# Perceiver block on Trainium2: cross-attentions with four-batch roots, summed head halves in the projection and joint key rotation

## The chip, the cores and the metric

The kernel runs on one NeuronCore of one Trainium2 chip. Its engines are TensorE (PE, with weight loads shown as PEld), VectorE (DVE), ScalarE (ACT), GpSimd (POOL) and SyncE (SP, which issues most DMAs). The metric is the device time of one execution in microseconds; lower is better.

## The reference

A block of six residual stages works on x of shape 32 x 32 x 256 (32 batches of 32 tokens). Two stages are cross-attentions to a context of 257 tokens for each batch, with 16 heads of 16 channels. These two are what the change touches.

```python
# stage 1: biases on q, k, v, o, and a mask
scores = q @ k^T / 4 + mask * -1e9          # per batch and head: 32 x 257
x = x + softmax(scores) @ v @ Wo + bo
# stage 4: no bias, no mask; q and k normed over 16 channels, then rotated
q = rope(q * rsqrt(mean(q*q) + eps) * wq);  k = rope(k * rsqrt(mean(k*k) + eps) * wk)
x = x + softmax(q @ k^T / 4) @ v @ Wo
```

Between and behind them stand a compressed self-attention with a Fourier transform, a plain self-attention and two layers of eight experts. All is float32.

## The kernel before, in words

Every engine has its own instruction stream, and the order in each is written by hand; semaphores join them. `cross(l)` is there for each engine, for the first (`l == 0`) and the second (`l == 1`) cross-attention. Its work goes in slots, one for each batch b = 4n + j (n = 0..7 groups of 128 tokens, j = 0..3). The two groups at each end are written out, and the ones between run in a hardware loop. In slot b the engines work on several batches at once, by the distances in `KEYS_AHEAD` and the constants beside it.

PE in slot b, in this order: turns probabilities of b, first half (`turns`, L685); scores of b+1 (`scores`, L671, which I use as the start of a slot); in slots with j = 1 the output projection of the four batches of group n-1 (`project`, L719); keys of a later batch, first half (`keys`, L617); `turns`, second half; `keys`, second half; for l = 1 the rotated keys of b+2 (`turn_keys`, L633, twice); values of b+1, first half (`values`, L649); weighted values of b (`weigh`, L702 and L706); `values`, second half. The two halves go through two PSUM banks, 6 and 7. Each matmul row of the trace holds two records for one matmul with 256 columns.

DVE in slot b: `merge` of b-1, which reads bank 5, where `weigh` left two head halves (L1560 multiplies by the share, L1563 adds the two halves, L1565 adds the value of the last, 257th context token); `shares` (L1539, L1542); for j = 1 `added` (L1572, the projection onto x, and L1578, statistics); `maxima` of b+1 (L1524 and L1528 for l = 0, L1530 for l = 1); then the copies of keys and probabilities out of PSUM (L1588, L1552, L1588). For l = 1 follow the sums of squares (L1601), every second slot the 12-step inverse root of two batches (L1630 to L1636), and the norm (L1619). A projection waits until `merge` of the batch with j = 0 of the next group has read bank 5, since it writes the same bank.

The context differs from its last token by `differ` (L2034, POOL), and POOL rotates keys for l = 1 (`rotate`, L1997 to L2001, four instructions for each half). ACT does exponentials (L1217) and the other copies. Before the slots of l = 0, DVE adds the output bias to x (L1656). The keys of the first batches of l = 1 are made early, while the results of the experts are gathered.

## Time and profile before

| | |
|---|---|
| median of three runs | 1277.69 us (1276.63 to 1279.93) |
| the profiled execution: its own time | 1276.58 us |
| its span in the profile | 1274.7 us |
| PE busy in the span | 996.5 us (78%) |
| DVE, ACT, POOL busy | 607.9, 494.9, 335.0 us |
| first cross-attention | from the start to about 251 us |
| second cross-attention | its early keys from 596 us, its slots from 675 to 951 us |

A busy share is a mean over stages with different limits. For a stage with slots, the length of one slot against the busy time of each engine in it says more: an engine that is busy for the whole slot sets its length, and where none is, the order of waits does.

### The profile page before, as it was taken

What the parts mean: (1) busy time and instruction counts of PE and PEld (TensorE: products, weight loads), DVE (VectorE), ACT (ScalarE), POOL (GpSimd) and SP (SyncE); (2) the same over time, 40 slices, a digit from 0 to 9 for tenths busy, and PEclk for the clock granted to TensorE, in tenths of its full rate; (3) what the DMA queues carried; (4) which work ended last, traced back from release to release, by engine and by line L of the source; (5) the groups of instructions that cost most, each with busy time, mean ns of one, the idle gap of its engine ahead of it and who ended that gap; (6) DMA issues with size and microseconds to landing.
All of it is one profiled execution on the core that took longest, in us unless ns stands there. A gap on an engine that the chain in (4) does not pass through costs nothing.

```text
span 1274.7 us, 24294 instructions
## 1 busy us (share of the span) xinstructions
PE 996.5 (78%) x8506; PEld 794.9 (62%) x8506; DVE 607.9 (48%) x1835; ACT 494.9 (39%) x1442; POOL 335.0 (26%) x494
## 2 busy tenths in 40 slices
PE   5999999888873899998147888888768875199990
PEld 3677667544652799997135656565548764199980
DVE  4555666513634011112775888888744554022222
ACT  3665666533330333322134555555545652011100
POOL 3111120002104000003527776777602100400004
PEclk9899999988985899999578999999986776599995
DMA  8111124000004788883100001100000000679953
GB/s 247 35 35 35 61 82 149 2 1 0 1 1 190 260 336 316 330 325 120 29 33 18 30 24 35 34 33 1 2 1 1 1 0 1 225 288 334 329 214 100
DMA packets 50562, 135.75 MB, mean 106 GB/s; under 512 B 16168, under 2 KB 37552, under 8 KB 44464
## 3 DMA queue, kind: packets, MB, share of 16 engines
q1 hardware_dynamic: 47408, 126.28, 27.8%
q0 software_dynamic: 3072, 8.39, 2.0%
q8 instruction: 49, 0.80, 0.2%
q14 instruction: 33, 0.27, 0.1%
HBM read 117.36 MB, written 17.30 MB: 106 GB/s over the span
## 4 chain that ended last, share of the span: by engine, by line
PE 60%; DVE 22%; issue 7%; ACT 3%; POOL 3%; SPq 2%; DMA 2%; DVEq 0%; another core or an unknown queue 0%; POOLq 0%; ACTq 0%
PE lower L1091 13%; PE upper L1100 9%; PE upper L649 6%; PE upper L617 5%; PE upper L850 3%; PE upper L685 3%; PE lower L671 2%; POOL xslot L2144 2%; PE upper L702 2%; PE lower L831 2%; PE upper L931 2%; DVE arena L1552 2%; PE upper L719 2%; DVE x L1960 1%; PE lower L566 1%
## 5 line engine op out<-in xcount | busy, mean ns | idle before, releaser
L1091 PEld LDWEIGHTS lower<-arena 128*128 128x128 f32 x1472 | 175.0, 195 | 6.1 <-DVE arena L1926 3.9
L1091 PE MATMUL lower<-arena 128*128 128x128 f32 x1472 | 176.0, 279 | 2.6 <-DVE arena L1926 2.6
L649 PE MATMUL upper<-wkv,arena 128*128 128x256 f32 x512 | 140.4, 398 | 12.0 <-ACT arena L1192 6.8
L1100 PE MATMUL upper<-arena 128*128 128x256 f32 x552 | 126.4, 379 | 0.0
L2150 POOL DMA_INDIRECT arena<-yslot,slot x32 | 30.7, 958 | 323.5 <-DMA yslot<-arena 314.3
L649 PEld LDWEIGHTS upper<-wkv,arena 128*128 128x128 f32 x512 | 90.5, 192 | 34.6 <-issue 12.3
L1100 PEld LDWEIGHTS upper<-arena 128*128 128x128 f32 x552 | 101.5, 190 | 12.0
L1450 ACT ACTIVATE arena<-lower,arena 128x128 f32<-128x128 f32 x184 | 52.5, 369 | 106.3 <-PE lower L1091 106.3
L1217 ACT ACTIVATE arena<-lower,arena 128x257 f32<-128x257 f32 x128 | 59.6, 474 | 60.2 <-DVE arena L1530 60.2
L2034 POOL TENSOR_TENSOR arena<-arena 128x512 f32<-128x512 f32 x64 | 70.6, 1114 | 36.4 <-ACT klast L1270 20.7
L685 PE MATMUL upper<-const,arena 128*128 128x128 f32 x512 | 77.8, 275 | 1.7 <-ACT arena L1227 1.4
L617 PE MATMUL upper<-wkv,arena 128*128 128x256 f32 x256 | 72.0, 412 | 6.3 <-DMA arena<-in_ctxT_dram 4.3
L1926 DVE COPY arena<-lower 128x256 f32<-128x256 f32 x46 | 19.3, 420 | 117.2 <-PE lower L1075 117.2
L685 PEld LDWEIGHTS upper<-const,arena 128*128 128x128 f32 x512 | 64.1, 142 | 17.1 <-ACT arena L1227 4.5
L617 PE MATMUL upper<-arena,wkv 128*128 128x257 f32 x256 | 68.6, 392 | 0.6 <-ACT vlast L1158 0.6
L1217 ACT ACTIVATE arena<-arena 128x257 f32<-128x257 f32 x128 | 63.7, 500 | 11.5 <-DVE arena L1528 10.9
L1203 ACT ACTIVATE arena<-upper 128x256 f32<-128x256 f32 x128 | 48.8, 381 | 48.5 <-PE upper L649 48.4
L2144 POOL DMA_INDIRECT xslot<-xn,slot x32 | 31.1, 973 | 133.1 <-DVE slot L1910 67.7
L1939 DVE COPY arena<-upper 128x256 f32<-128x256 f32 x46 | 19.5, 425 | 96.3 <-PE upper L1100 96.3
L617 PEld LDWEIGHTS upper<-wkv,arena 128*128 128x128 f32 x256 | 47.8, 203 | 21.0 <-issue 15.7
L566 PE MATMUL lower<-const,xn 128*128 128x128 f32 x96 | 20.4, 393 | 50.4 <-DVE xn L1499 50.4
L633 PE MATMUL upper<-const,arena 128*128 128x128 f32 x128 | 26.8, 299 | 38.1 <-DVE arena L1588 37.7
(236 smaller groups left out, 1885.1 us busy)
## 6 DMA issues: line engine op xcount, KB each, us to landing
arena<-in_ew_dram SPq DMA_DIRECT2D x23, 2048.0 KB, 7.2
arena<-in_ew_dram SPq DMA_DIRECT2D x23, 1536.0 KB, 6.1
arena<-in_ctxT_dram SPq DMA_DIRECT2D x16, 1028.0 KB, 5.1
xslot<-zero SPq DMA_DIRECT2D x2, 2944.0 KB, 15.4
arena<-xslot SPq DMA_DIRECT2D x46, 128.0 KB, 5.9
yslot<-arena SPq DMA_DIRECT2D x46, 128.0 KB, 6.2
const<-in_const_dram SPq DMA_DIRECT2D x1, 1154.0 KB, 7.6
x<-in_x_dram SPq DMA_DIRECT2D x1, 1024.0 KB, 5.7
```

Source lines behind the costliest of these rows:

```text
L566: ins = nc.tensor.transpose(bank[b][:, (2 * t + c) * P:(2 * t + c + 1) * P], xn[:, 2 * b + t, c * P:c * P + P], ident)
L617: ins = mm(o, a, v, start=(c == 0), stop=(c == KC - 1))
L649: ins = mm(bank[6 + w][:, 0:D], dctx[k2][:, c, j2, w * P:w * P + P], wkv[l][:, c, D:2 * D], start=(c == 0), stop=(c == KC - 1))
L685: ins = nc.tensor.transpose(bank[4][:, i * P:i * P + P], prob[j % 2][:, i, w * P:w * P + P], ident)
L850: ins = mm(bank[4 + j][:, c * 8 * T:(c + 1) * 8 * T], vq[k][:, j, c * P:c * P + P], spT[k][:, 2 * c:2 * c + 2, :], start=True, stop=True)
L1091: ins = mm(bank[1 + half][:, i * P:i * P + P], ew[k][:, at:at + P], exT[k % 2][:, c, :], start=(c == 0), stop=(c == KC - 1))
L1100: ins = mm(bank[4 + k % 2][:, 0:D], eh[k % 2][:, i, :], ew[k][:, at:at + D], start=(i == 0), stop=(i == nh - 1))
L1203: A(vb[j2 % 2][:, w, :], bank[6 + w][:, 0:D], copy).then_inc(q["vc"], 1)
L1217: A(prob[j2 % 2][:, i, :], src, ACT.Exp, bias=negmax[j2 % 2][:, i:i + 1], accum_out=rowsum[j2 % 2][:, i:i + 1]).then_inc(q["probs"], 1)
L1450: ins = A(eh[k % 2][:, c, :], bank[1 + half][:, i * P:i * P + P], ACT.Gelu_apprx_tanh, bias=eb1[k][:, c:c + 1])
L2034: G.tensor_tensor(dctx[k2][:, :, j2, :], of[:, :, 0:LASTKEY], of[:, :, LASTKEY:S].to_broadcast([P, KC, LASTKEY]), ALU.subtract).then_inc(q ...
L2144: G.indirect_dma_start(out=xslot[l], out_offset=at(i, t), in_=xn[:, t, :], in_offset=None)\
```

## The change

It makes seven edits. (1) `merge` is one multiplication: the two head halves are no longer added, but both are multiplied by the output weights and summed in PSUM, so a projection has four matmuls in place of two. (2) The last token's value is no longer added in `merge`: before the slots, 16 matmuls (`last_outputs`) multiply all last values by the output weights, the result with the bias goes to the new tile `vwo`, and a fifth matmul with four contraction rows adds it in each projection. The bias is no longer added to x. (3) The root of the key norms is made once for four batches, keys are made eight slots ahead in place of six (`DIFF_AHEAD` and `SUMS_AHEAD` go to seven), and `kraw` is doubled. (4) POOL rotates both key halves with four instructions in place of eight. (5) PE makes the second half of the values ahead of `weigh`. (6) DVE does `shares` and `maxima` ahead of `merge`, and `added` after the copy of the turned probabilities; PE does the first half of the keys ahead of the projection. (7) One semaphore covers the last keys' load and the mask and bias loads.

```diff
-        KEYS_AHEAD = (2, 6)
-        DIFF_AHEAD = (2, 5)
-        SUMS_AHEAD, NORM_AHEAD, ROPE_AHEAD, TURN_AHEAD = 5, 4, 3, 2
+        KEYS_AHEAD = (2, 8)
+        DIFF_AHEAD = (2, 7)
+        SUMS_AHEAD, NORM_AHEAD, ROPE_AHEAD, TURN_AHEAD = 7, 4, 3, 2
...
+                def last_outputs():
+                    for b in range(4):
+                        for t in range(2):
+                            n = 2 * b + t
+                            for c in range(KC):
+                                ins = mm(bank[b][0:QB, t * D:t * D + D], vlast[l][:, c, QB * n:QB * n + QB], wo[l][:, c, :],
+                                         start=(c == 0), stop=(c == KC - 1))
+                        ins.then_inc(q["lastvals"], 1)
...
                     for c in range(KC):
-                        ins = mm(bank[5][:, 0:D], attended[k][:, c, :], wo[l][:, c, :], start=(c == 0), stop=(c == KC - 1))
-                    ins.then_inc(q["ow"], 1)
+                        for e in range(2):
+                            mm(bank[5][:, 0:D], attended[k][:, c, e, :], wo[l][:, c, :], start=(c == 0 and e == 0), stop=False)
+                    mm(bank[5][:, 0:D], const[0:QB, C_TOKB:C_TOKB + P], vwo.rearrange("j n d -> j (n d)")[:, bass.ds(n * D, D)],
+                       start=False, stop=True).then_inc(q["ow"], 1)
...
 # PE, slot
                     scores(n, k, j, it)
+                    keys(n, k, j, it, 0)
                     if there(n):
                         project(n, k, j)
-                    keys(n, k, j, it, 0)
...
                     values(n, k, j, it, 0)
+                    values(n, k, j, it, 1)
                     weigh(n, k, j, it)
-                    values(n, k, j, it, 1)
...
 # DVE, merge
-                    V.tensor_tensor(pairs.rearrange("p c e q -> p (c e q)"), bank[5][:, 0:P], parts_of, ALU.mult)\
-                     .then_inc(q["merge"], 1)
-                    dve.wait_ge(q["merge"], 2 * b + 1)
-                    V.tensor_tensor(merged, pairs[:, :, 0, :], pairs[:, :, 1, :], ALU.add).then_inc(q["merge"], 1)
-                    dve.wait_ge(q["merge"], 2 * b + 2)
-                    V.tensor_tensor(attended[k][:, :, T * j:T * j + T], merged,
-                                    vlast[l][:, :, bass.ds(b, 1)].to_broadcast([P, KC, T]), ALU.add).then_inc(q["outc"], 1)
+                    V.tensor_tensor(attended[k][:, :, :, T * j:T * j + T],
+                                    bank[5][:, 0:P].rearrange("p (c e q) -> p c e q", c=KC, e=2),
+                                    parts_of.rearrange("p (c e q) -> p c e q", c=KC, e=2), ALU.mult).then_inc(q["outc"], 1)
...
 # DVE, slot
+                    shares(n, k, j, it)
+                    maxima(n, k, j, it)
                     if there(n0):
                         merge(n0, k0, j0)
-                    shares(n, k, j, it)
+                    keys(n, k, j, it, 0)
+                    turned(n, k, j, it)
                     if j == 1 and there(n) and not (isinstance(n, int) and n == 0):
                         added(n - 1)
-                    maxima(n, k, j, it)
-                    keys(n, k, j, it, 0)
-                    turned(n, k, j, it)
                     keys(n, k, j, it, 1)
...
 # before the slots of l = 0, DVE
-                    dve.wait_ge(mask_loaded, 16 * (QB + 1))
+                    dve.wait_ge(mask_loaded, 16 * (QB + 1 + KC))
                     mine(V.tensor_scalar(negmask[:, :], negmask[:, :], -1e9, None, ALU.mult))
-                    for t in range(NT):
-                        ins = V.tensor_tensor(x[:, t, :], x[:, t, :], bo_bc[:, :], ALU.add)
-                    mine(ins)
+                    for b in range(4):
+                        dve.wait_ge(q["lastvals"], b + 3)
+                        V.tensor_tensor(vwo[:, 2 * b:2 * b + 2, :], bank[b][0:QB, :].rearrange("j (n d) -> j n d", d=D),
+                                        bo_bc[0:QB, :].unsqueeze(1).to_broadcast([QB, 2, D]), ALU.add).then_inc(q["vwc"], 1)
```

How instructions stand on PE before, in the slot of batch 5 (j = 1) of the first cross-attention, from its scores on; arena holds the working tiles, upper and lower are the PSUM banks 4 to 7 and 0 to 3:

```order
L671 MATMUL lower<-arena 64x257 x8
L719 MATMUL upper<-wo,arena 128x256 x2
L617 MATMUL upper<-arena,wkv 128x257 x2
L685 MATMUL upper<-const,arena 128x128 x4
L617 MATMUL upper<-arena,wkv 128x257 x2
L649 MATMUL upper<-wkv,arena 128x256 x2
L702 MATMUL upper<-arena 32x64 x16
L706 MATMUL upper<-const,arena 32x128 x4
L649 MATMUL upper<-wkv,arena 128x256 x2
```

And the same slot in the changed kernel, with its own line numbers:

```order
L680 MATMUL lower<-arena 64x257 x8
L624 MATMUL upper<-arena,wkv 128x257 x2
L729 MATMUL upper<-wo,arena 128x256 x4
L730 MATMUL upper<-vwo,const 128x256
L694 MATMUL upper<-const,arena 128x128 x4
L624 MATMUL upper<-arena,wkv 128x257 x2
L656 MATMUL upper<-wkv,arena 128x256 x4
L711 MATMUL upper<-arena 32x64 x16
L715 MATMUL upper<-const,arena 32x128 x4
```

The projection (L719, now L729 and L730) has five matmuls in place of two and stands behind the first keys; all values stand ahead of the weighing.

On DVE before, around the merge that this projection waits for (L1560 to L1565), up to the first of the maxima of the same slot (L1522, L1524):

```order
L1552 COPY arena<-upper 128x512
L1560 TENSOR_TENSOR arena<-upper,arena 128x128
L1563 TENSOR_TENSOR arena<-arena 128x64
L1565 TENSOR_TENSOR arena<-arena,vlast 128x2x32
L1539 RECIPROCAL arena<-arena 128x4
L1542 TENSOR_TENSOR arena<-const,arena 128x128
L1572 TENSOR_TENSOR x<-x,upper 128x256
L1578 BN_STATS ln_stats<-x 128x6
L1522 MEMSET spare 1x1
L1524 ISA arena<-lower,negmask 128x257
```

And in the changed kernel, from the second half of that slot's maxima on:

```order
L1540 MEMSET spare 1x1
L1542 ISA arena<-lower,negmask 128x257
L1542 ISA arena 128x1
L1542 ISA arena<-lower,negmask 128x257
L1542 ISA arena 128x1
L1546 TENSOR_SCALAR arena<-arena 128x2
L1578 TENSOR_TENSOR arena<-upper,arena 128x4x32
L1570 COPY arena<-upper 128x512
L1586 TENSOR_TENSOR x<-x,upper 128x256
L1592 BN_STATS ln_stats<-x 128x6
```

The merge, now one instruction (L1578), stands behind all maxima of the slot, and the addition to x behind the copy of the turned probabilities.

## Rows read from the trace of the kernel before

**Rows 1.** Stretches, first cross-attention: length; busy PE, PEld, DVE, ACT, POOL; clock; DMA.

```profile
124.20:132.02 7.82, 7.08 (x85) 5.38 (x84) 4.38 (x21) 4.35 (x15) 0.00 (x0) 1.00 0.33 107
132.02:139.24 7.22, 6.23 (x82) 4.63 (x81) 4.92 (x19) 4.56 (x15) 5.19 (x6) 1.00 0.09 33
139.24:145.39 6.15, 6.15 (x82) 4.60 (x81) 3.63 (x18) 4.27 (x15) 0.00 (x0) 1.00 0.01 4
69.53:239.62 170.09, 160.80 (x2029) 120.77 (x2028) 102.63 (x465) 108.73 (x351) 26.98 (x31) 1.00 0.20 68
```

**Rows 2.** The same view, second cross-attention.

```profile
825.73:837.09 11.36, 7.96 (x90) 5.66 (x89) 8.22 (x23) 4.77 (x16) 8.04 (x14) 1.00 0.15 45
844.27:852.94 8.67, 7.02 (x86) 4.90 (x85) 6.90 (x17) 4.76 (x16) 7.59 (x14) 1.00 0.00 0
852.94:860.04 7.10, 6.80 (x85) 4.97 (x84) 6.72 (x17) 4.75 (x16) 5.35 (x9) 1.00 0.00 0
683.36:894.15 210.79, 178.97 (x2121) 128.54 (x2120) 176.63 (x457) 118.97 (x376) 152.07 (x260) 0.99 0.08 26
894.15:946.83 52.68, 39.12 (x517) 26.88 (x516) 32.83 (x86) 27.48 (x88) 20.27 (x37) 0.94 0.01 2
```

**Rows 3.** Timeline of PE, first cross-attention: start, length, work, idle before.

```profile
124.81 1.13 PE L719 MATMUL upper<-wo,arena 128*128 128x256 f32 x4
...
140.83 0.60 PE L685 MATMUL upper<-const,arena 128*128 128x128 f32 x4
141.26 1.03 PE L617 MATMUL upper<-arena,wkv 128*128 128x257 f32 x4
142.13 1.03 PE L649 MATMUL upper<-wkv,arena 128*128 128x256 f32 x4
```

**Rows 4.** Timeline of DVE, the same slot as the last three rows.

```profile
142.17 0.69 DVE L1552 COPY arena<-upper 128x512 f32<-128x512 f32 x1
144.35 0.29 DVE L1560 TENSOR_TENSOR arena<-upper,arena 128x128 f32<-128x128 f32 x1 [1.49 <-ACT arena L1235]
```

**Rows 5.** Timeline of PE and DVE, second cross-attention.

```profile
806.35 0.44 PE L633 MATMUL upper<-const,arena 128*128 128x128 f32 x2 [0.30 <-DVE arena L1588]
...
806.92 0.20 DVE L1630 TENSOR_SCALAR root_v<-arena 128x64 f32<-128x64 f32 x1
...
809.94 0.69 DVE L1619 TENSOR_TENSOR arena<-arena 128x512 f32<-128x512 f32 x1
...
822.70 0.89 DVE L1630 TENSOR_SCALAR root_v<-arena 128x64 f32<-128x64 f32 x1
...
828.69 1.13 PE L719 MATMUL upper<-wo,arena 128*128 128x256 f32 x4 [2.27 <-DVE arena L1565]
...
829.98 0.42 DVE L1572 TENSOR_TENSOR x<-x,upper 128x256 f32 x1 [0.86 <-PE upper L719]
```

**Rows 6.** Timeline of the program's start, and of the last keys' matmuls.

```profile
22.10 0.99 PE L578 MATMUL upper<-ctxl,wkv 128*128 128x32 f32 x8
...
24.31 1.09 DVE L1654 TENSOR_SCALAR negmask<-negmask 128x257 f32<-128x257 f32 x1 [11.10 <-DMA bo_bc<-in_bo_dram]
...
25.43 6.86 DVE L1656 TENSOR_TENSOR x<-x,bo_bc 128x256 f32<-128x256 f32 x8
...
28.50 1.28 ACT L1217 ACT_TABLE_LOAD   x1
...
34.85 2.07 PE L649 MATMUL upper<-wkv,arena 128*128 128x256 f32 x4 [5.15 <-ACT arena L1171]
...
590.97 1.05 PE L585 MATMUL upper<-wkv,ctxl 128*32 128x256 f32 x4
```

**Rows 7.** Timelines around the second cross-attention: POOL and PE.

```profile
669.01 0.46 POOL L1997 TENSOR_TENSOR arena<-arena,ropew 128x128 f32<-128x128 f32 x1 [15.59 <-DVE arena L1619]
...
673.75 1.19 POOL L2040 TENSOR_TENSOR arena<-qT,const 128x256 f32<-128x256 f32 x2
...
916.06 1.48 PE L649 MATMUL upper<-wkv,arena 128*128 128x256 f32 x4 [2.73 <-ACT arena L1192]
```

More of the change, by code:

```diff
@@ L245, in perceiver_block @@
         vb = [ar.take(KW2, D) for _ in range(2)]
-        kraw = [ar.take(KW2, D) for _ in range(QB)]
+        kraw = [[ar.take(KW2, D) for _ in range(QB)] for _ in range(2)]
         ksq = [ar.take(KW2, D) for _ in range(2)]
@@ L249, in perceiver_block @@
         krope = [ar.take(KW2, D) for _ in range(2)]
-        ka = ar.take(D)
-        kb = ar.take(D)
+        ka = ar.take(KW2, D)
+        kb = ar.take(KW2, D)
         lraw, lsq = ar.take(D), ar.take(D)
-        kss = ar.take(2 * KW2, NH)
-        kr = ar.take(2 * KW2, NH)
+        kss = ar.take(QB * KW2, NH)
+        kr = ar.take(QB * KW2, NH)
         lss, lr = ar.take(NH), ar.take(NH)
         assert ar.at < 21024
+        probT = [ar.take(KW2, 4, P) for _ in range(2)]
+        parts_of = ar.take(P)
+        assert ar.at < 21536
         ar.at = 21536
         xq = [ar.take(KC, QB, 2, T) for _ in range(2)]
-        attended = [ar.take(KC, P) for _ in range(2)]
+        attended = [ar.take(KC, 2, P) for _ in range(2)]
         prob = [ar.take(4, S) for _ in range(2)]
@@ L262, in perceiver_block @@
         xsmall = ar.take(64)
-        ar.at = 18000
-        probT = [ar.take(KW2, 4, P) for _ in range(2)]
-        pairs = ar.take(KC, 2, T)
-        merged = ar.take(KC, T)
-        parts_of = ar.take(P)
-        assert ar.at < 21024
         negmax = [xsmall[:, 4 * i:4 * i + 4] for i in range(2)]
@@ L665, in scores @@
                         after(pe, q["probs"], 4 * b2)
+                    if isinstance(b2, int) and b2 == 0:
+                        pe.wait_ge(q["vwc"], 4)
                     if j2 == 0:
@@ L747, in cross @@
                     last_values()
[L748 removed]
+                    pe.wait_ge(q["lastvals"], 2)
                     pe.wait_ge(q["qc"], 4)
+                    last_outputs()
                     slots(pe, slot, -KEYS_AHEAD[l])
@@ L768, in cross @@
                     turn_last_keys()
+                    last_outputs()
                     slots(pe, slot, 1 - EARLY, -1)
                     pe.wait_ge(q["qrope"], 1)
+                    pe.wait_ge(q["vwc"], 4)
                     for b in range(4):
@@ L1246, in slot @@
                     values(n, k, j, it, 0)
+                    values(n, k, j, it, 1)
                     shared(n, k, j, it)
-                    values(n, k, j, it, 1)
                 if l == 0:
@@ L2010, in rotate @@
                     after(pool, q["tw"], KW2 * (b2 - 1))
-                    for w in range(KW2):
-                        after(pool, q["krope"], KW2 * b2 + w)
-                        rope(krope[j2 % 2][:, w, :], kn[j2 % 2][:, w, :], P, rope_k(w), "krope", KW2 * b2 + w + 1)
+                    after(pool, q["krope"], b2)
+                    rope(krope[j2 % 2], kn[j2 % 2], P, 0, KW2, "krope", b2 + 1)
                 def last_column(n, k, j, it):
```

68 lines of the change are left out of this document (35 added, 33 removed).

## The prediction, made before the changed kernel ran

> **What bounds the kernel now.** I read the view of busy time by stretch first, with stretches cut from one batch's scores to the next. In the first cross-attention a plain slot takes 6.15 us and PE is busy for 6.15 of them: PE alone sets it. The slot with j = 1 takes 7.82, and j = 2, where POOL works 5.19 us beside it, 7.22; PE has gaps there [rows 1]. So a group of four takes 27.3 us, of which PE's stream is 4 x 6.15 + 0.97 for the projection. In the second cross-attention a group takes 34.2 us (11.36, twice some 7.1, and 8.67) and PE is busy for only about 28 [rows 2]. There the timeline shows PE waiting for DVE: 2.27 us ahead of the projection, 0.30 ahead of the turned keys, and more in slots that follow a root [rows 5]. DVE's long pieces there are the roots, 3.02 us from the first step to the norm where nothing disturbs them [rows 5]. So an edit that shortens DVE pays in the second cross-attention, and one that lengthens PE, or puts something ahead of what PE waits for, costs in the first.
>
> **First cross-attention, slots.** Times are from the start of a slot's scores.
>
> The projection: two matmuls with 256 columns stand 0.87 apart from the next two (141.26 to 142.13), so one is 0.435, and 0.10 is added where short matmuls follow [rows 3]. Five are 2.27, where two are 0.97: +1.30. The fifth has only four contraction rows. Its price is not in the trace; I bound it between nothing and 0.435 and take 0.435, since its columns are those of the others. The Trainium skill, "TensorE: Matmul & The Clock Gate" (Why this matters for your kernels), says that a single matmul with 32 contraction rows takes the time of one with 128; by it the sum stays as it is, and no row here shows it for four rows. If it were free, 14 projections would return 6 us.
>
> Its wait: before, `merge` is long done, and the projection starts 0.61 after the scores (124.81) [rows 1, 3]. Now the merge follows the maxima. These end 2.93 into the slot (142.17 less 139.24), the multiplication is 0.32 with its gap (0.29 busy), and DVE to PE takes about 0.14: the projection starts at 3.4 [rows 1, 4]. The first keys, moved ahead of it, cover PE only until 1.59 (140.83) [rows 3]. So PE idles 1.8. The values are now four long matmuls in a row, which saves one change of 0.10. The slot is 6.15 - 0.10 + 2.27 + 1.8 = 10.1, in place of 7.7 in the mean (170.09 less five of 7.22 and 13 of 6.15, over seven). Nothing hides this: turns, keys, values and weighing all stand behind the projection on PE.
>
> The j = 2 slot: before, weighing waited for DVE's copy of the turned probabilities, which now comes 0.32 later (merge in between), but no second half of the values follows the weighing: 7.22 + 0.32 - 0.97 = 6.6. The other slots: 6.05. There the copy ends at about 3.9 and PE reaches the weighing at 4.7, so moving the merge costs nothing; without that cover it would cost 0.3 a slot.
>
> From slot 5 to slot 30 (170.09 us, 25 slots) there are seven projections, five j = 2 slots with POOL's burst and 13 others: 7 x 10.1 + 5 x 6.6 + 13 x 6.05 = 182.4: **+12.3** [rows 1]. The last projection's five matmuls (+1.3) are met by two DVE instructions fewer (-0.6) and two slots without values behind the weighing (-0.7): 0.
>
> **First cross-attention, start.** Now DVE's additions to x (6.86 us until 32.3) hold the first maxima, and the first exponential starts 1.0 later, at 33.3 [rows 6]. They go. But PE's last values move from 22.10 behind the bias load (24.3), and 16 matmuls of 0.435 follow (7.0; the two of the last keys, with 32 columns of weights, took 1.05). ACT's table load came 6.4 after the last values' start (28.50); now it comes at 24.3 + 7.0 + 6.4 = 37.7 and ends 1.28 later, so the first exponential is at 39.0: +5.7 [rows 6]. Against it: PE idled 5.15 us before 34.85, and its next matmuls ran at half pace (2.07 where 1.03 is usual) with the turns and scores behind them I put the loss at 2.2 [rows 3, 6]. The 16 matmuls fill that gap. Net **+3.5** (bounds +1.6, if the table is loaded before the keys' copy, and +5.7).
>
> **Second cross-attention.** Early keys: two batches more. PE's four groups at 0.87 are 3.5, and the root, now over 128 elements, costs 0.8 more (a step on 64 elements is 3.02 / 12 = 0.25 with its gap, one on 128 is 0.32, as the multiplication of the merge) [rows 3 to 5]. DVE goes on to the experts' sum only after this work: **+4.3** (0 if the gathers were the later, 9 if the stalls between the early copies grow with them).
>
> Handover: POOL waited 15.59 us and began a rotation at 669.01, behind the root that DVE made after the queries; its eight instructions took until 673.75, and only then were the queries spread that the first scores need [rows 7]. That root (3.0) is now made early, and the joint rotation takes some 4.0 in place of 4.74: **-3.8** (0 to -4.3). POOL's start after the last keys' copy moves by 7 us of `last_outputs` and of four copies, under DVE's work on the queries.
>
> Slots: no root in j = 2 any more, so j = 3 falls from 8.67 to the others' length. A plain slot: DVE's merge is 0.32 later than the maxima, but its copies had waited for PE, so PE's second turned keys move only by 0.16; behind them 0.10 is saved: 7.15, as now (7.10) [rows 2, 5]. j = 1: the root starts at 4.3 of the j = 0 slot and takes 3.8, the norm 0.6: until 1.55 of the next slot. Shares 0.7, maxima 1.2, merge 0.3: the projection starts at 3.85 (2.96 now, 828.69) and takes 2.27. Then a turn 0.44, its copy on DVE 0.7, the addition with statistics 0.95 (two instructions on 256 elements; the first is 0.42), the key copy 0.5, and 3.44 of PE behind it (a plain slot, 7.15, less the 3.7 at which its second turned keys start): 12.1, against 11.36 [rows 2, 5]. The 25 slots of 210.79 us become 5 x 12.1, one of 8.5 (root, no projection), 18 x 7.15 and one of 6.2 (keys are done sooner): 203.9: **-6.9** [rows 2]. Of the last stretch (52.68) the stall of 2.73 before 916.06, which the last root caused, goes with its cold clock (-3.3), two projections grow (+1.2 and +2 at the lower clock), and ends shrink by 1.0: **-1.1** [rows 2, 7].
>
> **Sum.** 12.3 + 3.5 + 0 + 4.3 - 3.8 - 6.9 - 1.1 = +8.3, against the profiled execution's own 1276.58: 1284.9. That execution lies 1.1 under the median, so 1286.
>
> **Rivals.**
> 1. The second cross-attention becomes bound by PE (faster). DVE's work in a group falls from 28.4 busy by about 5; if its copies then always came ahead of PE, a slot is PE's own 6.7 (7.10 less the wait of 0.30 and the 0.10 saved) and all 25 take 25 x 6.7 + 5 x 2.27 = 179 in place of 204: 1261 [rows 2, 5]. For it: roots are what delays the j = 3 slot. Against: PE's second turned keys still stand behind scores, maxima, merge and two copies of their own slot. It decides where 12 of those 25 us come, with a plain slot at 6.9 or less and no wait ahead of the projections. That half gives 1274.
> 2. The preludes cost nothing (no change). If the last outputs and the early keys lie in gaps that exist anyway (5.15 us of PE idle at the start, the gathers of the experts' results), 7.8 goes: 1278.
> 3. Longer POOL instructions hold DVE up (slower yet). One root step took 0.89 beside a POOL instruction where it takes 0.20 [rows 5]. I expect POOL to be through before the root starts; if not, about 1.2 for each of six roots: 1293. The Trainium skill, "SBUF — State Buffer" (SBUF: two separate sides), says that DVE and GpSimd take a shared port pair for a whole instruction, and the other waits; the 0.89 agrees, and by it joint rotations of over 1 us make each collision longer.
>
> **Numbers.** Forecast 0.50; rival 1 0.18; rival 2 0.17; rival 3 0.15. Predicted time 1286. The range of 1273 to 1295 takes in rival 2, rival 3 and the bounds of the preludes, and leaves most of rival 1 out. What a measurement tells from no change here is 0.3%, 3.8 us. Slower 0.65 (forecast and rival 3), same 0.17, faster 0.18.
>
> **What would show it.** In the changed profile: first cross-attention j = 1 slots of 10 us with PE idle some 1.8 ahead of L729, released by DVE's L1578; its other slots at 6.05; the first exponential near 39 us; in the second, j = 1 near 12.1, j = 3 near 7.15, and the projection 3.9 after the scores. The forecast is wrong if the projections of the first cross-attention start within 2 us of their scores, if the five matmuls take well under 2.2 us, or if plain slots of the second fall below 6.9.

## The result and the profile after

The changed kernel takes 1294.43 us in the median of 4 runs (1290.01 to 1295.11), the kernel before 1277.16 (4 runs, 1273.87 to 1279.93): a ratio of 1.0129, 95% interval 1.0095 to 1.0162. The change makes the kernel 17 us slower. The forecast was slower by 8 (1286, range 1273 to 1295).

The view of busy time by stretch, the changed kernel, cut from scores to scores as before; first the slot of batch 13 (j = 1), the j = 2 slot behind it, a plain one, and the 25 slots from the sixth on, all of the first cross-attention:

```profile
core 0: us, PE busy (x) PEld busy (x) DVE busy (x) ACT busy (x) POOL busy (x), PEclk, DMA share, GB/s
133.19:143.39 10.20, 8.87 (x91) 6.20 (x90) 3.97 (x18) 4.44 (x14) 0.00 (x0) 1.00 0.17 53
143.39:149.99 6.60, 6.38 (x82) 4.53 (x81) 4.91 (x16) 4.43 (x14) 5.18 (x6) 1.00 0.21 83
156.34:162.52 6.18, 6.18 (x81) 4.52 (x80) 3.18 (x16) 4.29 (x14) 0.00 (x0) 1.00 0.00 0
75.07:259.01 183.94, 173.97 (x2072) 124.83 (x2071) 92.51 (x414) 109.41 (x350) 26.96 (x31) 1.00 0.18 63
```

Against [rows 1] the j = 1 slot is 10.20 in place of 7.82, the j = 2 slot 6.60 in place of 7.22, and the 25 slots 183.94 in place of 170.09. The timeline of the j = 1 slot (start, duration, engine, line; in brackets the idle time before it and its releaser) shows why:

```profile
135.93 0.29 DVE L1578 TENSOR_TENSOR arena<-upper,arena 128x128 f32<-128x128 f32 x1
...
136.27 2.00 PE L729 MATMUL upper<-wo,arena 128*128 128x256 f32 x8 [1.33 <-DVE arena L1578]
...
138.20 0.69 PE L730 MATMUL upper<-vwo,const 4*128 x2
...
138.82 0.66 PE L694 MATMUL upper<-const,arena 128*128 128x128 f32 x4
```

The projection starts 3.08 after its scores, released by the merge (L1578), which now stands behind the maxima; its five matmuls hold PE until the next turn at 138.82, 2.55 us. The second cross-attention, the same view: the slot of batch 1, a j = 1 slot, a plain one, the slot of batch 25, and the 25 slots from the first on:

```profile
713.38:723.74 10.36, 8.57 (x85) 5.80 (x84) 8.05 (x16) 4.75 (x15) 8.48 (x10) 0.84 0.01 2
778.76:791.07 12.31, 9.53 (x96) 6.63 (x95) 6.98 (x18) 4.75 (x15) 7.21 (x9) 1.00 0.01 1
798.20:805.38 7.18, 6.76 (x85) 4.90 (x84) 4.41 (x10) 4.75 (x15) 5.69 (x8) 1.00 0.40 133
914.24:929.87 15.63, 12.13 (x88) 8.19 (x87) 6.77 (x16) 4.34 (x14) 7.31 (x9) 0.67 0.00 0
706.32:914.24 207.92, 184.79 (x2143) 132.93 (x2142) 140.56 (x336) 118.72 (x376) 133.46 (x161) 0.98 0.07 24
```

The 25 slots are 2.9 shorter than in [rows 2] (210.79): the j = 3 slots are 7.1 in place of 8.67, the j = 1 slots 12.3 in place of 11.36, and the last stretch is longer (below).

Where the 17.3 us between the two profiled spans (1274.7 and 1292.0) lie, cut at PE's landmarks in both timelines (scores, and the transposes behind each layernorm):

| Stretch | before | after | difference | forecast |
|---|---|---|---|---|
| start, to the sixth slot's scores | 69.53 | 75.07 | +5.5 | +3.5 |
| first cross-attention, 25 slots | 170.09 | 183.94 | +13.9 | +12.3 |
| its end, to the transposes | 20.08 | 20.33 | +0.2 | 0 |
| first self-attention | 113.28 | 111.43 | -1.9 | 0 |
| experts, to the last values | 217.09 | 217.10 | 0 | 0 |
| last values and early keys, to the transposes | 43.75 | 51.96 | +8.2 | +4.3 |
| queries, to the first slot's scores | 49.54 | 46.49 | -3.1 | -3.8 |
| second cross-attention, 25 slots | 210.79 | 207.92 | -2.9 | -6.9 |
| its last slots, to the transposes | 56.38 | 58.39 | +2.0 | -1.1 |
| second self-attention | 116.86 | 112.05 | -4.8 | 0 |
| the rest | 207.31 | 207.32 | 0 | 0 |

The two self-attention stages are the same code in all kernels here. Over the 14 profiles of this study the first takes 111.4 to 116.1 and the second 111.1 to 116.9, without any tie to the edits: I take -1.9 and -4.8 for that spread and not for a gain of the change. With one profile of each kernel this is not settled.

### The profile page after: what moved, and what is told of

It reads as the page before. It is cut to its first block, busy times and chain, and to the rows that moved or that the text cites. A ratio compares the mean times of both kernels' runs of the same rounds, so it can differ in the third digit from the quotient of the medians.

```text
span 1292.0 us, 24163 instructions
## 1 busy us (share of the span) xinstructions
PE 1040.5 (81%) x8666; PEld 814.5 (63%) x8666; DVE 542.8 (42%) x1607; ACT 497.8 (39%) x1446; POOL 316.9 (25%) x366
## 4 chain that ended last, share of the span: by engine, by line
PE 63%; DVE 15%; issue 10%; POOL 4%; ACT 4%; SPq 2%; DMA 1%; another core or an unknown queue 1%; DVEq 0%; POOLq 0%; ACTq 0%
PE lower L1105 13%; PE upper L1114 9%; PE upper L656 7%; PE upper L694 4%; PE upper L624 4%; PE upper L729 3%; PE lower L680 3%; PE upper L711 3%; PE upper L864 2%; DVE arena L1548 2%; PE upper L945 2%; PE lower L845 1%; DVE arena L1602 1%; DVE arena L1736 1%; ACT arena L1351 1%
## 5 line engine op out<-in xcount | busy, mean ns | idle before, releaser
L656 PE MATMUL upper<-wkv,arena 128*128 128x256 f32 x512 | 126.5, 388 | 7.1 <-ACT arena L1206 4.4
L656 PEld LDWEIGHTS upper<-wkv,arena 128*128 128x128 f32 x512 | 93.7, 192 | 25.7 <-ACT arena L1185 6.8
L694 PE MATMUL upper<-const,arena 128*128 128x128 f32 x512 | 82.0, 283 | 2.0 <-ACT arena L1241 1.4
L624 PE MATMUL upper<-wkv,arena 128*128 128x256 f32 x256 | 74.0, 422 | 11.9 <-issue 5.3
L2049 POOL TENSOR_TENSOR arena<-arena 128x512 f32<-128x512 f32 x64 | 66.0, 1043 | 48.9 <-ACT klast L1288 33.4
L694 PEld LDWEIGHTS upper<-const,arena 128*128 128x128 f32 x512 | 57.5, 142 | 27.4 <-issue 17.8
L624 PEld LDWEIGHTS upper<-wkv,arena 128*128 128x128 f32 x256 | 48.6, 208 | 30.2 <-issue 21.9
L1570 DVE COPY arena<-upper 128x512 f32<-128x512 f32 x64 | 43.6, 682 | 51.6 <-PE upper L694 51.6
L1548 DVE TENSOR_REDUCE arena<-lower 128x2 f32<-128x514 f32 x64 | 41.3, 686 | 55.3 <-PE lower L680 55.3
L1542 DVE CUSTOM_DVE_ANT_0 arena<-lower,negmask 128x257 f32<-128x257 f32 x128 | 49.0, 420 | 27.5 <-PE upper L694 24.0
```

Source lines behind the costliest of these rows:

```text
L624: ins = mm(o, a, v, start=(c == 0), stop=(c == KC - 1))
L656: ins = mm(bank[6 + w][:, 0:D], dctx[k2][:, c, j2, w * P:w * P + P], wkv[l][:, c, D:2 * D], start=(c == 0), stop=(c == KC - 1))
L694: ins = nc.tensor.transpose(bank[4][:, i * P:i * P + P], prob[j % 2][:, i, w * P:w * P + P], ident)
L1542: V.tensor_tensor_reduce(prob[p][:, i, :], bank[i][:, 0:S], negmask[:, :], 1.0, float(np.finfo(np.float32).min), ALU.add, ALU.max, rowmax[ ...
L1548: V.tensor_reduce(negmax[p][:, two], lower[:, two, 0:S], AX_X, ALU.max, negate=True)\
L1570: V.tensor_copy(probT[j % 2][:, 1, :, :].rearrange("p i q -> p (i q)"), bank[4][:, :]).then_inc(q["turnc"], 1)
```

## The experiments

All were timed in turns with the kernel before on the same chip; a ratio below 1 is faster than before. The kernel before took 1274.38 in the turns of the first four kernels of the table and 1276.8 to 1277.0 in the others, so kernels of different turns are best compared by their ratios. "Slots" is the time from the first slot's scores to those of the 26th in the second cross-attention (before 210.79, after 207.92).

| Kernel | median us | ratio, 95% interval | slots |
|---|---|---|---|
| the change, merge first | 1264.33 | 0.9926 (0.9901 to 0.9950) | 195.46 |
| the change, two matmuls | 1267.89 | 0.9953 (0.9934 to 0.9972) | 200.26 |
| before, keys' part | 1306.98 | 1.0256 (1.0233 to 1.0279) | 237.90 |
| before, values' order | 1278.43 | 1.0032 (1.0013 to 1.0052) | 215.09 |
| before, joint rotation | 1308.40 | 1.0239 (1.0213 to 1.0266) | 240.93 |
| before, root per four | 1266.06 | 0.9926 (0.9899 to 0.9953) | 202.57 |
| hybrid | 1249.32 | 0.9784 (0.9766 to 0.9802) | 195.45 |
| merge first, four early | 1268.11 | 0.9928 (0.9907 to 0.9949) | 195.36 |
| hybrid, separate rotation | 1254.19 | 0.9817 (0.9785 to 0.9850) | 197.22 |
| joint rotation, merge in PSUM | 1263.04 | 0.9898 (0.9869 to 0.9928) | 203.49 |
| hybrid, late gathers | 1253.27 | 0.9814 (0.9786 to 0.9841) | 195.59 |
| before, root per four and order | 1259.82 | 0.9878 (0.9845 to 0.9912) | 206.19 |

### 1. Is it the merge's place? (the change, merge first)

```
 # DVE, slot
+                    if there(n0):
+                        merge(n0, k0, j0)
                     shares(n, k, j, it)
                     maxima(n, k, j, it)
-                    if there(n0):
-                        merge(n0, k0, j0)
                     keys(n, k, j, it, 0)
```

> The changed kernel with one edit: DVE does the merge's one multiplication first in a slot, ahead of the shares and the maxima, as the kernel before did; the five-matmul projection, its place behind the first keys and all else stay. Theory (the projections wait for the late merge): the first cross-attention's slots with a projection fall from 10.2 to 8.8 us (the projection starts 1.65 after its scores, when the first keys are through, in place of 3.08), 7 of them: -10; the second's fall from 12.3 to 10.9 where the root does not hold DVE longer, 6 of them: -8. Together 1276, within 3. Rival (the merge's place costs nothing in sum): the maxima of every slot come 0.3 later, exponentials and weighing with them, 60 slots of which half pay, and the result stays within 0.3% of the changed kernel's 1294.

Measured 1264.33: 30 us less than the changed kernel (27 when each is set against the kernel before of its own turns), and faster than before. Busy time by stretch (the slot of batch 13, a j = 1 slot and batch 25's of the second cross-attention, its 25 slots), and PE's projection in the timeline of batch 25:

```profile
131.83:140.44 8.61, 8.61 (x92) 6.29 (x91) 3.98 (x19) 4.44 (x14) 0.00 (x0) 1.00 0.20 60
770.19:780.88 10.69, 9.53 (x96) 6.63 (x95) 7.14 (x17) 4.75 (x15) 7.21 (x9) 1.00 0.01 2
896.89:905.90 9.01, 7.65 (x87) 5.28 (x86) 5.74 (x14) 4.23 (x14) 5.90 (x8) 1.00 0.00 0
701.43:896.89 195.46, 181.82 (x2143) 131.18 (x2142) 140.84 (x337) 118.74 (x376) 131.89 (x161) 1.00 0.08 26
```

```profile
898.69 1.99 PE L729 MATMUL upper<-wo,arena 128*128 128x256 f32 x8 [1.11 <-DVE arena L1578]
```

In the first cross-attention the j = 1 slot falls by 1.6 and PE is busy for all of it. In the second it falls by 1.6 too. The plain slots are 7.06 for the most part (7.09 before this edit). The rival's price isn't paid there: the merge starts 0.14 before the slot's scores, in time in which DVE stood anyway, and the maxima start as long after the scores as before the edit (the last of them after 1.41 in plain slots of the second cross-attention). Only in its j = 1 slots, where the root holds DVE until then, do most of them come 0.7 later. The gain is 12 us beyond the expectation: the slots of batch 1 and 21 fall by 1.8 and 3.3 (their clock is no longer under 0.9), and above all the slot of batch 25 takes 9.01, not 15.63. In the changed kernel its projection looks like this:

```profile
916.10 0.83 DVE L1560 TENSOR_TENSOR arena<-const,arena 128x128 f32<-128x128 f32 x1
916.86 1.28 DVE L1548 TENSOR_REDUCE arena<-lower 128x2 f32<-128x514 f32 x2
918.06 0.27 DVE L1578 TENSOR_TENSOR arena<-upper,arena 128x128 f32<-128x128 f32 x1
...
918.39 3.78 PE L729 MATMUL upper<-wo,arena 128*128 128x256 f32 x8 [3.45 <-DVE arena L1578]
...
922.10 1.22 PE L730 MATMUL upper<-vwo,const 4*128 4x256 f32 x2
```

PE idles 3.45 us, and its next matmuls go at half pace: 3.78 where 2.00 is usual (granted clock 0.67 over the slot, so most of it at 1.2 GHz, the lower of the two levels). With the merge first PE idles 1.11 there, and the clock stays at 1.00. So here the wait is paid twice, once as idle time (2.3 of the 6.6 us) and again in the matmuls behind it: from batch 25's scores to the transposes behind the layernorm the changed kernel takes 58.39 and this one 51.01. The second price is not fixed by the length of the wait, as the next kernel shows.

### 2. What do three matmuls cost? (the change, two matmuls)

```
-                        for e in range(2):
-                            mm(bank[5][:, 0:D], attended[k][:, c, e, :], wo[l][:, c, :], start=(c == 0 and e == 0), stop=False)
-                    mm(bank[5][:, 0:D], const[0:QB, C_TOKB:C_TOKB + P], vwo.rearrange("j n d -> j (n d)")[:, bass.ds(n * D, D)],
-                       start=False, stop=True).then_inc(q["ow"], 1)
+                        ins = mm(bank[5][:, 0:D], attended[k][:, c, 0, :], wo[l][:, c, :], start=(c == 0), stop=(c == KC - 1))
+                    ins.then_inc(q["ow"], 1)
```

> The changed kernel with a projection of two matmuls: it leaves out the second halves of the heads and the last values with the output bias (the merge's product for both halves, the last outputs and all waits stay). It measures what three more matmuls cost. Theory (PE has nothing beside them, everything in the slot stands behind): 2.55 falls to 0.97, so -1.58 for each of 16 projections: -25, to 1269. Rival (in the second cross-attention DVE sets the slot, so the matmuls are hidden there): only the first's 8 projections pay, -12.6, to 1282.

Measured 1267.89. The first cross-attention's j = 1 slots fall from 10.20 to 8.58, the full 1.6. In the second they are 10.86, 11.73, 10.58 and 11.79 in place of 12.49, 12.31, 12.22 and 12.25: two of four fall by the full 1.6, two by a third of it. The stretches of batch 9, 13 and 25 tell why:

```profile
767.15:778.88 11.73, 9.57 (x90) 6.85 (x89) 7.09 (x18) 4.76 (x15) 7.21 (x9) 0.85 0.00 0
800.28:810.86 10.58, 7.89 (x90) 5.66 (x89) 6.94 (x18) 4.76 (x15) 7.21 (x9) 1.00 0.01 4
896.62:907.70 11.08, 7.58 (x81) 5.42 (x80) 6.77 (x16) 4.24 (x14) 6.11 (x8) 0.85 0.01 1
```

```profile
900.76 1.86 PE L728 MATMUL upper<-wo,arena 128*128 128x256 f32 x4 [3.45 <-DVE arena L1576]
```

The two longer slots have a granted clock of 0.85 and 0.86, where the changed kernel had 1.00: they save the three matmuls too, and lose 1.1 of it to the clock. So the matmuls are not hidden in the second cross-attention. Batch 25's slot is 11.08 in place of 15.63, of which the three matmuls are only a part. PE waits 3.45 for the merge as in the changed kernel, and the clock falls behind it here too (1.86 for two matmuls that take 1.13 elsewhere), but for less long: 0.85 over the slot, not 0.67. That brings the last stretch from 58.39 to 51.67, and the total near the expected 1269 is in part this luck. The same wait was thus followed by a short and by a long time at the lower clock, and a wait of 1.86 ahead of batch 9's projection by none in the changed kernel and by some here. What decides it, the runs don't show.

### 3. What is the keys' part worth? (before, keys' part; joint rotation; root per four)

The first of the three puts both edits into the kernel before, the other two one each: `KEYS_AHEAD` 8 with `DIFF_AHEAD` and `SUMS_AHEAD` 7 and `kss`, `kr` and the root over `QB * KW2`, or the rotation

```
-                    for w in range(KW2):
...
-                        rope(krope[j2 % 2][:, w, :], kn[j2 % 2][:, w, :], P, rope_k(w), "krope", KW2 * b2 + w + 1)
...
+                    rope(krope[j2 % 2], kn[j2 % 2], P, 0, KW2, "krope", b2 + 1)
```

> The kernel before with the keys' part of the change alone: keys eight batches ahead, one root per four batches, both halves of a batch's keys rotated together. Theory: the early keys cost 8 to 9 more (two more batches in straight-line code beside the gathers), the handover to the queries gives 2 to 4 back, and in the second cross-attention the j = 3 slots lose 1.5 each (six of them: -9) while the root ahead of j = 1 grows by 0.8 (+5) and the tail gives 3: in sum 1275 to 1280, no difference that can be told. Rival A (POOL's longer instructions hold DVE's roots up): 1285 or more. Rival B (the keys' part is the good part, and the early keys' cost is met elsewhere): 1270 or less.

> The kernel before with one part of the change: both halves of a batch's keys are rotated together on POOL (four instructions of up to 1.27 us in place of eight shorter ones); keys stay six ahead, a root per two batches. Theory (a POOL instruction holds up DVE's instructions that have both operands and the result in SBUF, for as long as it runs; the joint ones are longer and fall on DVE's merge and shares): the second cross-attention's slots grow, though by less than in the kernel with eight keys ahead, 0.5 to 1 in each of 25: 1285 to 1300. Rival (the joint rotation is shorter in sum and harmless, the loss of the kernel with all of the keys' part came from the root over four batches or from keys eight ahead): 1272 to 1277.

> The kernel before with the other part: keys eight batches ahead and one root per four batches; the halves of the keys are still rotated one after the other. Theory (the joint rotation is what made the keys' part 32 us slower): early keys +9, fewer roots -9, root ahead of j = 1 +5, handover -2: 1278 to 1284. Rival (the root over four batches, or where it falls against POOL's work, is the cause): 1295 or more.

Measured 1306.98, 1308.40 and 1266.06. The two halves of the same part have opposite signs: the joint rotation alone costs 31 us, the root per four batches alone gives 11. With both, the kernel is as slow as with the first, so that beside roots per four batches the joint rotation costs over 40. None of the three theories was met in size: "no difference" for the sum was wrong by 30 us, the joint rotation cost more than its 0.5 to 1 a slot (1.2), and the roots per four gave 11 where a small loss was expected. The time of the first is that of its rival A, but not for rival A's reason: in its slots no root step takes over 0.3. The groups of instructions of DVE in the slots show what happens (mean ns behind the comma): first the kernel before, then the joint rotation.

```profile
L1542 DVE TENSOR_TENSOR arena<-const,arena 128x128 f32<-128x128 f32 x25 | 13.9, 556 | 1.0
L1565 DVE TENSOR_TENSOR arena<-arena,vlast 128x64 f32<-128x64 f32 x24 | 9.3, 387 | 2.3
L1563 DVE TENSOR_TENSOR arena<-arena 128x64 f32<-128x64 f32 x24 | 8.0, 332 | 0.8
```

```profile
L1542 DVE TENSOR_TENSOR arena<-const,arena 128x128 f32<-128x128 f32 x25 | 25.6, 1026 | 1.0
L1565 DVE TENSOR_TENSOR arena<-arena,vlast 128x64 f32<-128x64 f32 x24 | 21.4, 892 | 2.3
L1563 DVE TENSOR_TENSOR arena<-arena 128x64 f32<-128x64 f32 x24 | 21.0, 874 | 0.8
```

The shares (L1542) and the merge's two additions (L1563, L1565) are the same instructions on the same tiles, and take 1.8 to 2.6 times as long. DVE's busy time in the 25 slots rises from 176.63 to 206.13, by 29.5; the slots grow by 30.1. The timeline of one slot of the kernel with joint rotations sets the two engines side by side:

```profile
833.23 0.73 POOL L1999 TENSOR_TENSOR arena<-arena,ropew 128x256 f32<-128x256 f32 x1 [6.99 <-DVE arena L1619]
833.24 0.80 DVE L1563 TENSOR_TENSOR arena<-arena 128x64 f32<-128x64 f32 x1
...
833.91 0.73 POOL L2000 TENSOR_TENSOR arena<-arena,ropew 128x256 f32<-128x256 f32 x1
...
834.16 0.56 DVE L1565 TENSOR_TENSOR arena<-arena,vlast 128x64 f32<-128x64 f32 x1
...
834.60 1.27 POOL L2001 TENSOR_TENSOR arena<-arena,ropew 128x512 f32<-128x512 f32 x1
834.64 0.17 DVE L1539 RECIPROCAL arena<-arena 128x4 f32<-128x4 f32 x1
834.84 1.17 DVE L1542 TENSOR_TENSOR arena<-const,arena 128x128 f32<-128x128 f32 x1
...
835.94 1.28 DVE L1530 TENSOR_REDUCE arena<-lower 128x2 f32<-128x514 f32 x2
835.95 1.26 POOL L2003 TENSOR_TENSOR arena<-arena 128x512 f32<-128x512 f32 x1
```

Each of the three DVE instructions ends with the POOL instruction beside it (834.04 and 833.96, 834.72 and 834.64, 836.01 and 835.87), while the reduction out of PSUM (two of 0.64) takes its usual time beside L2003. In the first cross-attention of the kernel before, where POOL rotates nothing, the additions are never held up:

```profile
L1565 DVE TENSOR_TENSOR arena<-arena,vlast 128x64 f32<-128x64 f32 x25 | 5.6, 226 | 2.3
L1563 DVE TENSOR_TENSOR arena<-arena 128x64 f32<-128x64 f32 x25 | 5.6, 225 | 0.8
```

The Trainium skill, "SBUF — State Buffer" (SBUF: two separate sides), says that DVE and GpSimd share one pair of ports as an exclusive lock, held for a whole instruction, and that a DVE instruction with two SBUF inputs contends for it with a GpSimd instruction that reads SBUF; by that rule the additions must wait and the reduction not, which is what the rows show.

### 4. Is it where the operands lie? (joint rotation, merge in PSUM)

```
+                    pairs = bank[5][:, 2 * P:3 * P].rearrange("p (c e q) -> p c e q", c=KC, e=2)
...
-                    V.tensor_tensor(merged, pairs[:, :, 0, :], pairs[:, :, 1, :], ALU.add).then_inc(q["merge"], 1)
+                    V.tensor_tensor(merged, pairs[:, :, 0, :],
+                                    vlast[l][:, :, bass.ds(b, 1)].to_broadcast([P, KC, T]), ALU.add).then_inc(q["merge"], 1)
...
-                    V.tensor_tensor(attended[k][:, :, T * j:T * j + T], merged,
-                                    vlast[l][:, :, bass.ds(b, 1)].to_broadcast([P, KC, T]), ALU.add).then_inc(q["outc"], 1)
+                    V.tensor_tensor(attended[k][:, :, T * j:T * j + T], pairs[:, :, 1, :], merged, ALU.add).then_inc(q["outc"], 1)
```

> The kernel with joint rotations alone (1308), with the merge's product in PSUM in place of SBUF, and its two additions ordered so that each reads one half of it there. Same instructions, same sizes, same queue order. Theory (DVE waits for POOL only with all operands in SBUF): the two additions fall from a mean of 0.85 and 0.89 us to 0.2 to 0.3 and the time to 1278 to 1290 (the shares are still held up). Rival (the slots grew since POOL's results come later or in another order, and the long DVE durations are only where a wait shows): no change, 1303 or more.

Measured 1263.04, 45 us less than with the product in SBUF and faster than the kernel before. The same groups as above:

```profile
L1542 DVE TENSOR_TENSOR arena<-const,arena 128x128 f32<-128x128 f32 x25 | 20.8, 832 | 1.0
L1564 DVE TENSOR_TENSOR arena<-upper,vlast 128x64 f32<-128x64 f32 x24 | 5.4, 225 | 2.3
L1567 DVE TENSOR_TENSOR arena<-upper,arena 128x64 f32<-128x64 f32 x24 | 5.4, 224 | 0.8
```

Both additions take 0.22 to 0.23 in every slot. POOL's instructions and their order in its queue are the same, so the loss did not come from how long or in what order POOL works; one operand in PSUM was enough. The shares, still all in SBUF, are still held up (0.83). The gain was larger than I expected, for two reasons that the rows give: the additions were held up in the kernel before as well (0.33 and 0.39 against 0.225), so this one falls below it (slots 203.49 against 210.79), and PE, which idles less, keeps its clock (granted 1.00 over the slots in place of 0.93).

This explains the changed kernel too, and what my forecast missed: the new merge is one instruction that reads PSUM (L1578, 0.27 to 0.28 in each of the 24 slots), so the joint rotation, worth +31 beside the old merge, did little beside it (section 6 has the pair of runs). Part (1) and part (4) of the change can't be costed apart.

### 5. The order of the values (before, values' order)

```
                     values(n, k, j, it, 0)
+                    values(n, k, j, it, 1)
                     weigh(n, k, j, it)
-                    values(n, k, j, it, 1)
```

ACT's copies of the values stand in the same order.

> The kernel before with one edit: both halves of the values stand together on PE and the weighing is last in a slot (and ACT's copies in that order). Theory: one change between short and long matmuls less, 0.1 in each plain slot of the first cross-attention, and 0.6 in each of its seven j = 2 slots, where the weighing waited for DVE's copy; nothing in the second, where DVE's copies set the slot: -6, to 1271. Rival (a late weighing makes DVE's merge, which is first in the next slot, wait, and the maxima behind it): the j = 1 slots and the plain ones grow, and the time is 1277 or more.

Measured 1278.43, 0.3% slower than before: the rival. The j = 2 slots of the first cross-attention do fall from 7.21 to 6.6 and the plain ones to 6.11, but j = 1 grows from 7.83 to 7.98 and some j = 3 from 6.15 to between 6.5 and 6.8, so its 25 slots stay (169.84). In the second, some slots reach 8.3 and the 25 grow by 4.3. That the merge, first on DVE, waits for a weighing that is now last is my reading of it; no run isolates it.

### 6. Good parts together (hybrid; separate rotation; root per four and order)

The hybrid is kernel 1, but in the first cross-attention with the old merge and projection and the output's bias added to x; there are no last outputs ahead of it.

```
+                    if l == 0:
+                        for c in range(KC):
+                            ins = mm(bank[5][:, 0:D], attended[k][:, c, 0, :], wo[l][:, c, :], start=(c == 0), stop=(c == KC - 1))
+                        ins.then_inc(q["ow"], 1)
+                        return
...
                     pe.wait_ge(q["qc"], 4)
-                    last_outputs()
                     slots(pe, slot, -KEYS_AHEAD[l])
```

> The changed kernel with the merge first in DVE's slot, and in the first cross-attention the old merge of three instructions and projection of two matmuls (no last outputs ahead of it, the output's bias added to x as before); the second keeps its projection of five. Theory (the first cross-attention is set by PE, so there the long projection and the last outputs only cost; the second is set by DVE): the start is 5 earlier than with the last outputs, the first's j = 1 slots fall from 8.6 to 7.9: 1264 - 5 - 5 = 1254, within 4. Rival (the start is set by something else, as the first exponential waits for ACT's table, and the three short DVE instructions push the maxima back): 1262 or more.

> The hybrid kernel (merge first, old projection in the first cross-attention, new one in the second) with the keys' halves rotated one after the other again. Theory (the joint rotation costs only through DVE's instructions that have all operands in SBUF; of the merge's three the new projection leaves one, which reads PSUM, so only the shares are still held up, 0.50 in place of 0.29): nothing of weight either way, 1247 to 1251. Rival A (the joint rotation still costs): 1245 or less. Rival B (it is a gain here, since POOL hands the keys over sooner): 1253 or more.

> The kernel before with keys eight ahead, a root per four batches, separate rotations, and the change's order but for the merge, which stays first: values together, weighing last, first keys ahead of the projection, additions to x behind the turned probabilities. It has no trace of the new projection. Theory (the new projection is worth nothing of itself once the rotations are separate; what the hybrid gains is roots and order): the first cross-attention gains its 6.4 as in the hybrid: 1266 - 6 = 1260, less what the order gives in the second: 1250 to 1260. Rival A (the new projection is needed in the second): 1262 or more, with plain slots over 7.3 as in the kernel with the values' order alone. Rival B (better than the hybrid): 1247 or less.

The hybrid is the fastest kernel here: 1249.32, 2.2% under the kernel before, and a little faster than expected, since its j = 1 slots are 6.97 where I had put 7.9.

```profile
71.00:234.65 163.65, 161.59 (x2029) 118.55 (x2028) 100.79 (x465) 110.08 (x350) 27.17 (x31) 1.00 0.21 71
683.57:879.02 195.45, 181.81 (x2143) 131.18 (x2143) 140.93 (x337) 118.73 (x376) 131.91 (x161) 1.00 0.08 26
```

Its sixth slot starts at 71.00 (76.76 with last outputs), and the first cross-attention's 25 slots take 163.65, 6.4 less than before: j = 1 is 6.97, with the first keys ahead of the projection and the addition to x behind the copy. With separate rotations it takes 1254.19, the time of rival B; the slots are 1.8 longer, the way from the early stage to them 2.6, and the intervals of the two ratios overlap a little, so that the joint rotation is a small gain here is likely, not settled. With the old merge in both cross-attentions and roots per four (1259.82) the first gains the same (163.7), but the second's slots are 206.19, not 197.22 as in the hybrid with separate rotations, with plain ones of 7.3 to 8.0: there the new merge and projection, which take two instructions off DVE, are worth 9 us of the slots. Of the whole they are worth less, 5.6 by the medians, and the intervals of the two ratios just overlap.

### 7. The early keys (merge first, four early; hybrid, late gathers)

`EARLY = 5` in place of 3, and in the other kernel one wait ahead of POOL's gathers:

```
+                if l == 0:
+                    pool.wait_ge(xs[1]["kw"], 12)
```

> The changed kernel with the merge first, and four batches' keys made early in place of six (the other two, and the root over the first four, come behind the queries). Theory (each early batch costs some 4.5 in code that runs once, while PE, ACT and DVE stand for 2.4 to 3.9 at a time): the early stage gives 9 back, the handover loses the root and two batches' keys, 4 to 6: 1264 - 4 = 1260. Rival (the queries' stage pays it all, since POOL's rotations then wait for the root): 1265 to 1270.

> The hybrid kernel in which POOL starts the gathers of the experts' results only when PE has made the six early batches of keys of the second cross-attention. Theory A (PE, ACT and DVE stand in the early stage because of the gathers' transfers): the early keys take 12 to 14 us in place of 24, the gathers (20 us) follow, and the time is 1255 to 1262. Theory B (they stand because this code runs once and is loaded as it runs): the early keys take 22 us or more as they do now, and the time is 1266 or more.

Four early batches in place of six take the 9.2 off this stretch (42.26, with six 51.46), and the way from there to the first slot grows by 11.4: nothing is gained, 1268.11, as the rival had it. The second kernel shows why six cost so much. PE's early keys, in the changed kernel and, behind it, in the hybrid with late gathers:

```profile
614.26 7.80 PE L624 MATMUL upper<-wkv,arena 128*128 128x256 f32 x28 [4.43 <-DVE arena L1679]
624.49 2.07 PE L624 MATMUL upper<-wkv,arena 128*128 128x256 f32 x4 [2.43 <-issue]
629.42 2.07 PE L624 MATMUL upper<-wkv,arena 128*128 128x256 f32 x4 [2.85 <-issue]
633.68 4.87 PE L624 MATMUL upper<-wkv,arena 128*128 128x256 f32 x12 [2.19 <-DVE arena L1602]
```

```profile
590.59 12.12 PE L627 MATMUL upper<-wkv,arena 128*128 128x256 f32 x48 [4.39 <-DMA arena<-in_ctxT_dram]
```

The same 24 matmuls (48 records) take 24.3 us beside POOL's 16 gathers and 12.12 without them, with no gap, though their code runs once in both. So the stalls belong to the gathers, as theory A had it; which resource they and the engines' instructions share, the runs don't tell. The time is not better (1253.27, the ratio 0.9814 against 0.9784), since the gathers' 20 us now begin later and the layernorm comes after them.

## Why the prediction was right, and where its sizes were off

The sign and the main place were right; the size was half of what came, 8 of 17 us. By its own steps:

- **First cross-attention, slots: +12.3, measured +13.9.** The mechanism is as described: the projection waits for the merge (kernel 1: 1.6 a slot) and three more matmuls cost 1.6 (kernel 2). The wait was smaller than said (start at 3.08, not 3.4; PE idle 1.33, not 1.8), and the five matmuls dearer: 2.55, not 2.27, since of the two short gaps around the fifth, at each change of tile shape, only one was priced, and at 0.10 where the rows give 0.19 each. The fifth matmul, of four rows, wasn't free: it is 0.62 from its start to the next turn, gap included. The two errors nearly cancel (10.2 for 10.1), and j = 2 (6.60) came as written. Nearly all of the 1.6 that are missing lies in the other 13 slots, which were put at 6.05 and are 6.11 to 6.35, 6.16 in the mean.
- **Start: +3.5, measured +5.5.** It lies close to the upper bound. The 16 matmuls ran in part at the lower clock (8.76 us, granted 0.81 over the stretch, where 7.0 was assumed), the last values ahead of them waited until 24.62 for the bias load, and the first exponential came at 41.09, where the forecast had 39.0 and the kernel before 33.34. The 2.2 that the filled gap gives back were right.
- **Early keys: +4.3, measured +8.2.** The failed step is "PE's four groups at 0.87 are 3.5": beside the gathers a batch costs 4.1 us in all, since PE stands between the keys, and without the gathers the stalls are gone (kernel with late gathers). The trace of before already showed such stalls among its early keys, and I kept them for the bound only:

```profile
605.58 0.42 DVE L1588 COPY arena<-upper 128x256 f32<-128x256 f32 x1 [2.70 <-PE upper L617]
606.06 2.07 PE L617 MATMUL upper<-wkv,arena 128*128 128x256 f32 x4 [1.98 <-issue]
```

- **Handover: -3.8, measured -3.1**, with the root gone from behind the queries as said.
- **Second cross-attention, slots: -6.9, measured -2.9.** j = 3 (7.1), plain (7.1 to 7.2) and j = 1 (12.3 for 12.1) are met. Missed are the slot of batch 1, 10.36 for 8.5, and the last j = 1 of the stretch, 13.91, both with a granted clock under 0.9.
- **Last stretch: -1.1, measured +2.0.** "+2 at the lower clock" was too little: behind the wait of 3.45 the granted clock was 0.67 over a whole slot of 15.63 (11.10 in the kernel before). Its projection starts 4.15 after the scores, and no keys are left there to fill PE's time, so PE idles 3.45 where the j = 1 slots before it have 1.8 to 2.2; the forecast didn't count that.
- **Rival 1** (bound by PE) needed plain slots at 6.9 or less; they are 7.1. **Rival 2** (free preludes) fell with 5.5 and 8.2. **Rival 3** was dismissed for the right kernel with the wrong reason: I looked at the roots, which POOL did leave alone but for two steps of 0.97 among the early keys. What POOL holds up is DVE's merge and shares. Had the change kept the old merge, rival 3 would have cost 30 us or more, not 7, by the kernels of section 3.

The sum of the misses in place (+2.0, +1.6, +3.9, +0.7, +4.0, +3.1) is 15: the stages that the change touches are 24 us longer in this pair of profiles, of a forecast of 8. The self-attention stages, which the forecast put at nothing, are 6.7 shorter and bring the total to 17. If that is their spread, it is in part luck that the time stayed within the range.

## What to carry to other kernels

Before merging small GpSimd instructions into longer ones, list VectorE's instructions beside them whose inputs both lie in SBUF: each can be held for the whole GpSimd instruction, and moving one operand to PSUM was worth 45 us here. Before you trust a sum of parts, cost them in the presence of each other, since a part worth +31 alone can be harmless beside another, and keep a short producer ahead of long work in its engine's queue when the bottleneck waits for it: one line's place was some 30 us. An edit that is right for a stage bound by VectorE (more matmuls, fewer vector instructions) is wrong for one bound by TensorE, even when both call the same function.

## What the runs showed of the hardware that was not expected

- A DVE addition of 128x64 took 0.22 to 0.23 us in all 24 slots with one input in PSUM, and 0.87 to 0.89 in the mean (up to 1.3) with both in SBUF, beside POOL instructions of up to 1.3 us.
- 24 matmuls of code that runs once took 24.3 us beside 16 gathers of POOL and 12.1 without; PE, ACT and DVE stood together, PE for 2.2 to 2.9 us at a time.
- A wait of PE of 3.45 us was followed by a granted clock of 0.67 over a slot of 15.6 us in one kernel and of 0.85 over one of 11.1 in another; with a wait of 1.11 in the same place the clock stayed at 1.00 and the slot was 9.0.
